# Causal attention with the row maximum carried in spare rows of the score product, and its masking moved to GpSimd

## The chip, the cores and the metric

The kernel runs as one program on one core of a Trainium2 chip. The metric is device time in microseconds of one execution, the median over the runs of the kernel. Engines: TensorE (PE in the rows; PEld is its weight load), VectorE (DVE), ScalarE (ACT), GpSimd (POOL) and the sync engine (SP), which issues the loads and stores.

## The reference, cut to what matters

The model has two layers over 16 sequences of 256 tokens, width 128. Layer 0 is a recurrence and a 64-expert network; layer 1 is attention and a 16-expert network. Only the attention of layer 1 is touched. Head width is 8, there are 16 heads, and since the rotary width is the whole width, only the rotary half of queries and keys is left:

```python
q_r = _apply_rope(x @ wqr + bqr, cos, sin)
k_r = _apply_rope(x @ wkr + bkr, cos, sin)
ckv = _gelu(x @ wkv + bkv)
v = (ckv @ wv + bv).reshape(b, s, H, HD).transpose(0, 2, 1, 3)
q, k = (_gelu(t).reshape(b, s, H, HD).transpose(0, 2, 1, 3) for t in (q_r, k_r))
scores = jnp.einsum('bhqd,bhkd->bhqk', q, k) / math.sqrt(HD)
scores = jnp.where(causal[None, None], -jnp.inf, scores)
attn = jax.nn.softmax(scores, axis=-1)
out = jnp.einsum('bhqk,bhkd->bhqd', attn, v)
return out @ wo + bo
```

## The kernel before, in words

The program runs layer 0, then the expert network of layer 1 (eight token tiles; it also leaves queries and keys in SBUF, feature by token, each split in a high part and a rest: `qh`, `ql`, `kh`, `kl`), then attention, one sequence ("batch") at a time. Every engine's queue is written out by hand and synchronised by named semaphores; nothing is scheduled by a tool. The attention loop is a software pipeline of three stages in each body `both(ba, bx, bo)`: stage A prepares batch b+2, stage X scores and averages batch b+1, stage O finishes batch b. Two parities alternate (`par`).

Stage A, `a_unit` (L1180 ACT, L1334 PE, L1614 DVE), goes through `UNITS` (L971), each unit into PSUM bank 0 or 1 by turns. Units `k` spread four heads at a time over the partitions: head j of a group of four sits on partitions 32j and following. 8 of the 32 partitions carry a head's high part, further ones repeat it or carry the rest, so that one product sums the split terms; the last 8 are spare. ScalarE copies the keys (`kr`, L1188). The query units do the same, and copies masked by `qmask` give each head an own copy of 128 partitions by 256 tokens (`qb`), zero outside its 32 partitions: eight heads by VectorE (L1623), eight by ScalarE (L1192). Units `max0` and `max1` compute scores with queries on partitions, two heads a unit, for the first and the second 128 queries, add the causal mask with a bf16 product of the identity and `mask_b`, and VectorE takes the row maximum (L1628). After the last one VectorE splits the maximum in two parts (`mhl`, L1631 and L1633), unit `mT` transposes them (L1367) and ScalarE copies them to `mT` (L1198).

Stage X: `scores_t` (L1371 and following) computes the transposed scores, keys on partitions, in eight units of two heads. Each of a unit's four quarters takes three products into one accumulation: keys by masked queries, `esel` by `mT` (which subtracts the row maximum), and the causal mask. Units alternate between two pairs of banks. ScalarE takes the exponential of 768 columns (L1204). `values` multiplies four heads' probabilities by values at once (L1398), into banks 6 and 7.

Stage O: ScalarE copies the raw output (L1210), TensorE transposes it (L1409), VectorE divides by the row sums (L1640, L1644), TensorE transposes (L1414), ScalarE copies (L1213), TensorE projects with `wo`, VectorE multiplies by the gate (L1649) and adds the residual (L1653). All plain products are recorded at the helper's line, L1239; the tiles tell them apart. `l_xt` and `l_wqk` hold `kr` of the two parities, `l_big` holds `qb`, the probabilities and small tiles, `l_rope` the raw output, `l_hid` the values.

GpSimd (`pool`, L1090 and following) sets constants, subtracts two splits for each token tile of the expert network and has nothing to do in attention. The sync queue loads layer 1's constants one after the other ahead of the first tile (L990), and the selectors `c_rep` and `c_esel` in four pieces during the last expert tile; VectorE casts each between experts (L1568).

## Time and profile before

| | |
|---|---|
| median of 3 runs | 2396.91 us (2391.91 to 2397.82) |
| profiled execution, own time | 2401.08 us |
| its span | 2399.3 us |
| mean granted TensorE clock | 0.882 |
| busy: TensorE, VectorE, ScalarE, GpSimd | 77%, 67%, 45%, 38% of the span |
| attention stage | 1890.6 us to the end |
| one batch in attention | 30.4 us |

The span is the stretch that the profile covers; the profiled execution's own time is 1.8 us longer. Busy time of TensorE counts overlapping matmuls once, and a matmul's recorded duration includes its way through the array; what one costs in a dense row of them is the distance between two starts. A granted clock of 1.00 is TensorE's higher level, 2.4 GHz; 0.5 would be 1.2 GHz throughout a stretch.

### The profile page before, as it was taken

The page shows a single profiled execution, that of the slowest core. Times are in us where ns is not written, and L with a number is a line of the kernel's source. Part 1 is how long each engine was busy: PE and PEld are TensorE (multiplying, and loading weights), DVE is VectorE, ACT ScalarE, POOL GpSimd, SP SyncE. Part 2 cuts the span into 40 slices and gives each one's busy share as a digit, 9 for nine tenths or more (in the row PEclk, how much of TensorE's full clock was granted, in tenths as well). Part 3 has the DMA queues.
Part 4 walks back from the last instruction along what each step waited for, and adds up shares of the span by engine and source line. Part 5 has one row for each costly group of instructions (what it writes and reads, how often), then busy time and mean ns, then how long its engine had stood idle before and what let it go on. Part 6 is the DMA issues. An engine that isn't in the chain of part 4 may idle for free. (4 is left out here: it accounts for less than half of the span.)

```text
span 2399.3 us, 35571 instructions
## 1 busy us (share of the span) xinstructions
PE 1837.1 (77%) x10242; PEld 1372.1 (57%) x10242; DVE 1615.1 (67%) x4233; ACT 1075.5 (45%) x1779; POOL 910.0 (38%) x729
## 2 busy tenths in 40 slices
PE   1384875866848768477486299898999999999998
PEld 1252553533525435244253288787888777777776
DVE  3599899898997989989989344444444444444443
ACT  2262553643625536355253155454455344444443
POOL 2776775757767667577486100000000000000000
PEclk8697887977978879789798599999999799999999
DMA  6220030200300203002000411111100100000000
GB/s 108 59 49 0 10 49 6 38 17 6 54 1 14 45 6 54 0 5 49 5 5 5 118 21 22 23 23 24 19 14 14 40 8 14 13 13 13 13 13 11
DMA packets 140839, 60.21 MB, mean 25 GB/s; under 512 B 94599, under 2 KB 135036, under 8 KB 140668
## 3 DMA queue, kind: packets, MB, share of 16 engines
q1 hardware_dynamic: 140668, 58.24, 12.0%
q8 instruction: 70, 1.15, 0.2%
q14 instruction: 101, 0.83, 0.1%
HBM read 37.10 MB, written 21.10 MB: 24 GB/s over the span
## 5 line engine op out<-in xcount | busy, mean ns | idle before, releaser
L554 PE MATMUL pb<-hid,wd 128*128 128x512 f32 x528 | 319.8, 691 | 215.6 <-POOL hid L391 211.0
L387 POOL TENSOR_TENSOR hid<-act_g,act_u 128x512 f32<-128x512 f32 x256 | 331.1, 1293 | 277.4 <-ACT act_c L481 260.1
L391 POOL TENSOR_TENSOR hid<-hid,act_c 128x512 f32<-128x512 f32 x256 | 332.7, 1300 | 20.1
L481 ACT ACTIVATE act_g<-pb 128x512 f32<-128x512 f32 (+1 forms) x264 | 158.5, 600 | 389.2 <-PE pb L504 386.1
L1239 PE MATMUL l_pb<-l_xt,l_big 128*128 128x512 f32 (+1 forms) x1024 | 299.4, 415 | 34.6 <-DVE l_rope L1518 24.1
L1586 DVE SCALAR_TENSOR_TENSOR l_acc<-l_pb,l_gtok,l_acc 128x128 f32<-128x128 f32 x512 | 144.0, 344 | 256.8 <-PE l_pb L1239 256.8
L502 PE MATMUL pb<-xt_hi,wg_hi 128*128 128x512 f32 (+1 forms) x264 | 223.9, 848 | 67.0 <-DMA wd<-in_L_ffn_Ws_down_dram 51.1
L554 PEld LDWEIGHTS pb<-hid,wd 128*128 128x128 f32 x528 | 96.6, 208 | 301.6 <-POOL hid L391 280.1
L1239 PEld LDWEIGHTS l_pb<-l_big,l_hid 128*128 128x128 f32 x2048 | 247.1, 192 | 10.6
L1628 DVE TENSOR_REDUCE l_mrow<-l_pb 128x2 f32<-128x256 f32 (+1 forms) x256 | 137.2, 556 | 171.9 <-PE l_pb L1239 168.9
L1167 ACT ACTIVATE l_hid<-l_pb,l_cols 128x512 f32<-128x512 f32 x256 | 169.4, 688 | 183.1 <-PE l_pb L1239 182.7
L1239 PE MATMUL l_pb<-l_big,l_hid 128*128 128x128 f32 x2048 | 247.9, 275 | 0.0
L1239 PEld LDWEIGHTS l_pb<-l_xt,l_big 128*128 128x128 f32 x1024 | 194.6, 200 | 73.0 <-DVE l_rope L1518 22.7
L756 DVE TENSOR_TENSOR products<-zr,rs 128x512 f32<-128x512 f32 x256 | 175.7, 686 | 23.7 <-POOL zr L340 10.4
L1204 ACT ACTIVATE l_big<-l_pb 128x768 f32<-128x768 f32 x128 | 104.6, 817 | 176.0 <-PE l_pb L1398 89.4
L502 PE MATMUL pb<-xt_hi,wu_hi 128*128 128x512 f32 (+1 forms) x264 | 116.3, 441 | 77.8 <-ACT act_g L481 77.7
L759 DVE TENSOR_REDUCE rs<-products 128x32 f32<-128x512 f32 x256 | 175.8, 687 | 0.0
L1105 POOL TENSOR_TENSOR l_ql<-l_rope,l_qh 128x512 f32 x8 | 10.3, 1289 | 434.5 <-ACT l_qh L1161 434.5
L757 DVE TENSOR_TENSOR products<-zr,rs 128x512 f32<-128x512 f32 x256 | 174.1, 680 | 0.0
L481 ACT ACTIVATE act_u<-pb 128x512 f32<-128x512 f32 (+1 forms) x264 | 158.1, 599 | 24.6 <-PE pb L504 16.5
L481 ACT ACTIVATE act_c<-pb 128x512 f32<-128x512 f32 x256 | 153.1, 598 | 0.0
L1239 PE MATMUL l_pb<-l_mT,l_esel 128*128 128x256 f32 x512 | 143.3, 280 | 0.0
(305 smaller groups left out, 4125.4 us busy)
## 6 DMA issues: line engine op xcount, KB each, us to landing
z_scratch<-zs SPq DMA_DIRECT2D x128, 81.0 KB, 4.2
zr<-z_scratch SPq DMA_DIRECT2D x8, 1296.0 KB, 8.4
x_sb<-in_L_attn_x_dram SPq DMA_DIRECT2D x32, 64.0 KB, 3.2
g_scratch<-act_u SPq DMA_DIRECT2D x8, 256.0 KB, 2.3
y_scratch<-yo SPq DMA_DIRECT2D x8, 256.0 KB, 2.3
l_xs<-in_L_attn_x_dram SPq DMA_DIRECT2D x32, 64.0 KB, 1.9
l_ys<-y_scratch SPq DMA_DIRECT2D x128, 16.0 KB, 1.7
l_gs<-g_scratch SPq DMA_DIRECT2D x8, 256.0 KB, 3.0
```

Source lines behind the costliest of these rows:

```text
L387: pool.tensor_tensor(hid1[:, :], g, u, ALU.mult).then_inc(s_h1, 1)
L391: pool.tensor_tensor(hid[:, p % 2, :], hid1[:, :], c, ALU.mult).then_inc(s_h, 1)
L481: act.activation(dst, pb[0:n, r % 4, :], ACT.Silu if what == 0 else ACT.Copy).then_inc(s_ev, 1)
L502: pe.matmul(out, l_hi, r_hi, start=first, stop=False, skip_group_check=True)
L554: last = pe.matmul(pb[:, 4, :], wd[0:n, p, :], hid[0:n, p % 2, :], start=(p == 0), stop=(p == PAIRS), skip_group_check=True)
L756: dve.tensor_tensor(products[:, 2:4], two(ZG), twice, ALU.mult).then_inc(s_st, 1)
L757: dve.tensor_tensor(products[:, 0:2], two(ZF), twice, ALU.mult).then_inc(s_st, 1)
L759: dve.tensor_reduce(rs[:, 3, 0:2], products[:, 2:4], AX.X, ALU.add).then_inc(s_st, 1)
L1167: act.activation(hid[:, r % HR, :], pb[:, 2 + r % 3, :], ACT.Relu, bias=cols[:, r:r + 1]).then_inc(s_hid, 1)
L1239: return pe.matmul(out, l, r, start=start, stop=stop, skip_group_check=True)
L1586: dve.scalar_tensor_tensor(out=acc[:, s, :], in0=pb[:, 5 + e % 2, sub], scalar=gtok[par][:, s, e:e + 1], in1=acc[:, s, :], op0=ALU.mult, o ...
L1628: dve.tensor_reduce(mrow[:, k, 2 * j:2 * j + 2], src, AX.X, ALU.max).then_inc(s_ua_dve, 1)
```

## The change

The masked copies change sides and engine. Queries are copied unmasked (`qr`) by VectorE; keys are copied by ScalarE with a bias `kspare` that puts -1 in two spare rows of each head's 32. GpSimd makes masked copies of the keys (`kb`, used by the maximum pass with four or two heads side by side in 512 columns) and of the queries (`qb`, used by the transposed scores). The maximum pass has twelve units instead of sixteen: for each group of four heads one with the first 128 queries and 128 keys of all four, and two with the second 128 queries and 256 keys of two heads; the mask is added in one product per unit. They use banks 2 and 3. The maximum's two parts are transposed to partitions 32j and 32j+1, in eight transposes, and copied straight into those rows of `qb`, groups j = 0 and 1 by ScalarE and j = 2 and 3 by VectorE. So the score product subtracts the maximum itself: `esel` and `mT` go, with their load, and so does the mask product. A score unit is one product of 512 columns (first 128 keys, two heads, all queries) and one of 256 (second 128 keys and queries), into banks 4 and 5 for every unit. The exponential is unchanged in size; after it GpSimd writes zeros above the diagonal with two `affine_select` per unit, and only then may `values` read. Ahead of each group of its work GpSimd does a one-column product on a small tile, the "turnstile".

```diff
         qb = [b[:, :].rearrange("p (h n) -> p h n", h=H1) for b in (big0, big1)]
-        kr = xt[0][:, :, :].rearrange("p a n -> p (a n)"), wqk[:, :, :, :].rearrange("p a j n -> p (a j n)")
+        GN = 4 * N
+        kr = xt[0][:, :, :].rearrange("p a n -> p (a n)"), wqk[:, :, :, :].rearrange("p a j n -> p (a j n)")[:, 0:GN]
+        qr = xt[1][:, :, :].rearrange("p a n -> p (a n)")
+        kb = sb("kb", [P, H1, N], F32R)
...
-        esel = sb("esel", [P, H1, P], F32R)
...
+        kspare = sb("kspare", [P, 1])
...
+        pt2 = sb("pt2", [P, 4, 3 * N])
         mrow = sb("mrow", [P, 2, H1])
-        mhl = sb("mhl", [P, 2, P], F32R)
-        mT = [sb(f"mT{i}", [P, N], F32R) for i in range(2)]
+        mhl = sb("mhl", [P, 2, H1, 32], F32R)
...
+        def probs(u):
+
+            p = (pt, pt2)[u // 4][:, u % 4, :]
+            return p[:, 0:2 * N].rearrange("p (m n) -> p m n", m=2), p[:, 2 * N:3 * N].rearrange("p (m n) -> p m n", m=2)
...
-        UNITS = ["k"] * 2 + ["q_dve", "q_act"] + ["max0"] * 8 + ["max1"] * 8 + ["v", "mT"]
+        UNITS = ["k0", "q0", "k1", "q1"] + ["max"] * 12 + ["v", "m"]
...
+        BY_ACT = [u in ("k0", "k1", "v") for u in UNITS]
+        BY_DVE = [u in ("q0", "q1", "max") for u in UNITS]
...
+        MAX0, NM, XU = 4, 12, 8
+        X_AT, V_AT = (2, 3, 5, 6, 8, 9, 11, 12), (7, 10, 13, 16)
+
+        O_RAW, O_TB, O_NORM, O_OT, O_WO, O_END = 0, 1, 2, 4, 5, 6
...
+        def max_rows(par, j):
+
+            rows = qb[par][32 * j:32 * j + 2, :, :].rearrange("p (g j) n -> p g j n", j=4)
+            return rows[:, :, j, :]
...
+            w(kspare[:, :], d["c_kspare"])
...
-            for i in range(4):
...
-                sp.dma_start(rep_stage, d[("c_rep", "c_esel")[i // 2]][:, STAGED * (i % 2):STAGED * (i % 2 + 1)]).then_inc(s_rep_ld, 16)
+                sp.dma_start(rep_stage, d["c_rep"][:, STAGED * i:STAGED * (i + 1)]).then_inc(s_rep_ld, 16)
...
+            def turn(n):
+                pool.wait_ge(s_turn, n)
+                pool.tensor_tensor(turnstile[:, 1:2], turnstile[:, 0:1], turnstile[:, 0:1], ALU.mult).then_inc(s_turn, 1)
...
+            def masked_keys(b, par, half, turns):
+
+                pool.wait_ge(*read(b, 2 * half))
+                turn(turns)
+                for j in range(4):
+                    at = slice(2 * N * half, 2 * N * (half + 1))
+                    out = kb[:, 8 * half:8 * (half + 1), :].rearrange("p (g j) n -> p g j n", j=4)[:, :, j, :]
+                    src = kr[par][:, at].rearrange("p (g n) -> p g n", n=N)
+                    last = pool.tensor_scalar(out, src.bitcast(F32), qmask[:, j:j + 1], None, ALU.mult)
+                last.then_inc(s_kb, 1)
...
+            def masked_queries(b, par, half, turns):
...
+            def causal(b, u, turns):
+
+                pool.wait_ge(s_pt, b * XU + u + 1)
+                turn(turns)
+                for k in range(2):
+                    diagonal = probs(u)[k][:, :, 0:P]
+                    last = pool.affine_select(diagonal, diagonal, pattern=[[0, 2], [1, P]], base=0, channel_multiplier=-1,
+                                              compare_op=ALU.is_ge, fill=0.0)
+                last.then_inc(s_cut, 1)
...
+            def both(ba, bx, pa, turns):
+                done = 0
+                for i in range(NU):
+                    if bx is not None and i - 1 in X_AT:
+                        causal(bx, X_AT.index(i - 1), turns + done)
+                        done += 1
+                    if ba is not None and i in (1, 2):
+                        masked_keys(ba, pa, i - 1, turns + done)
+                        done += 1
+                    if ba is not None and i in (8, 12):
+                        masked_queries(ba, pa, i // 12, turns + done)
+                        done += 1
...
+                if u[0] == "k":
+                    act.wait_ge(s_ua, b * NU + (i + 1))
+                    at = 2 * N * int(u[1])
+                    act.activation(kr[par][:, at:at + 2 * N], pb[:, BANK[i], :], ACT.Identity, bias=kspare[:, :]).then_inc(s_ua_act, 1)
...
+                elif u == "m":
+                    act.wait_ge(s_ua, b * NU + (i + 1))
+                    act.wait_ge(s_qb, (b + 1) * 2)
+                    for j in range(2):
+                        last = act.activation(max_rows(par, j), pb[32 * j:32 * j + 2, 0:2, :].rearrange("p a (g n) -> p (a g) n", n=N), ACT.Copy)
+                    last.then_inc(s_mq[0], 1)
...
             def x_unit(b, par, u):
+
                 act.wait_ge(s_st, b * XU + (u + 1))
-                act.wait_ge(s_pv, b * (XU // 2) + max(u // 2 - 1, 0))
-                at = 512 * (2 + 2 * (u % 2)) + N
-                act.activation(pt[:, u % 4, :], pbf[:, at:at + 3 * N], ACT.Exp, scale=float(1.0 / np.sqrt(HD1))).then_inc(s_pt, 1)
+                if u == 0:
+                    act.wait_ge(s_pv, b * 4)
+                p = (pt, pt2)[u // 4][:, u % 4, :]
+                act.activation(p, pbf[:, 4 * 512:4 * 512 + 3 * N], ACT.Exp, scale=float(1.0 / np.sqrt(HD1))).then_inc(s_pt, 1)
...
-                    if bx is not None and i % 2 == 0 and i // 2 < XU:
-                        x_unit(bx, px, i // 2)
+                    if bx is not None and i in X_AT:
+                        x_unit(bx, px, X_AT.index(i))
...
+                if u == "max":
+                    m = i - MAX0
+                    g, part = m // 3, m % 3
+                    if m >= 2:
+                        pe.wait_ge(*read(b, i - 2))
+                    if part == 0 and g % 2 == 0:
+                        pe.wait_ge(*read(b, g + 1))
+                        pe.wait_ge(s_kb, b * 2 + g // 2 + 1)
+                    bank = pb[:, 2 + m % 2, :]
+                    if part == 0:
+                        mm(bank.rearrange("p (j n) -> p j n", j=4), qr[:, N * g:N * g + P], kb[:, 4 * g:4 * (g + 1), 0:P], stop=False)
+                        last = mm(bank.rearrange("p (j n) -> p j n", j=4), ident_b[:, :], mask_b[:, :].unsqueeze(1).to_broadcast([P, 4, P]), start=False)
+                    else:
+                        h = 4 * g + 2 * (part - 1)
+                        mm(bank, qr[:, N * g + P:N * (g + 1)], kb[:, h:h + 2, :].rearrange("p h n -> p (h n)"), stop=False)
+                        last = mm(bank.rearrange("p (j n) -> p j n", j=2)[:, :, P:N], ident_b[:, :], mask_b[:, :].unsqueeze(1).to_broadcast([P, 2, P]), start=False)
+                    last.then_inc(s_ua, 1)
+                    return
+                bank = pb[:, BANK[i], :]
+                if u == "m":
+                    pe.wait_ge(s_mhl, b + 1)
+                    pe.wait_ge(*read(b, NU - 2))
+                    for h in range(0, H1, 4):
+                        for k in range(2):
+                            src = mhl[:, k, h:h + 4, :].rearrange("p j c -> p (j c)").bitcast(F32)
+                            at = N * (h // 4) + P * k
+                            last = pe.transpose(pbf[:, at:at + P], src, ident[:, :])
+                    last.then_inc(s_ua, 1)
+                    return
...
             def scores_t(b, par, u):
 
-
                 if u == 0:
-                    pe.wait_ge(s_ua_act, (b + 1) * N_ACT)
-                    pe.wait_ge(s_pt, b * XU)
-                elif u >= 2:
-                    pe.wait_ge(s_pt, b * XU + (u - 1))
-                bank = 512 * (2 + 2 * (u % 2))
-                for k, m, lo in ((1, 1, N), (1, 0, P), (0, 0, 2 * N), (0, 1, 3 * N)):
-                    h = 2 * u + m
-                    keys = N * (h // 4) + P * k
-                    out = pbf[:, bank + lo:bank + lo + N]
-                    mm(out, kr[par][:, keys:keys + P], qb[par][:, h, :], stop=False)
-                    mm(out, esel[:, h, :], mT[par][:, :], start=False, stop=False)
-                    last = mm(out[:, P * k:P * (k + 1)], mask_b[:, :], ident_b[:, :], start=False)
+                    for n in range(2):
+                        pe.wait_ge(s_mq[n], b + 1)
+                pe.wait_ge(s_pt, b * XU + u)
+                g, heads = u // 2, slice(2 * u, 2 * u + 2)
+                mm(pb[:, 4, :], kr[par][:, N * g:N * g + P], qb[par][:, heads, :].rearrange("p h n -> p (h n)"))
+                last = mm(pb[:, 5, 0:N].rearrange("p (m n) -> p m n", m=2), kr[par][:, N * g + P:N * (g + 1)], qb[par][:, heads, P:N])
                 last.then_inc(s_st, 1)
...
-            def values(b, par, u):
-
-                pe.wait_ge(s_pt, b * XU + (u + 2))
-                if u == 0:
+            def values(b, par, g):
+
+                pe.wait_ge(s_cut, b * XU + 2 * (g + 1))
+                if g == 0:
                     pe.wait_ge(s_done, b)
-                out = pb[:, 6 + u // 4, N * (u // 2 % 2):N * (u // 2 % 2 + 1)]
+                out = pb[:, 6 + g // 2, N * (g % 2):N * (g % 2 + 1)]
...
+                        p = probs(2 * g + m // 2)[k][:, m % 2, :]
+                        last = pe.matmul(out[VC * m:VC * (m + 1), P * k:N], vp[par][:, k, 4 * g + m, :], p, start=(k == 0), stop=(k == 1),
...
+                    if bx is not None and i in X_AT:
+                        scores_t(bx, px, X_AT.index(i))
+                    if bx is not None and i in V_AT:
+                        values(bx, px, V_AT.index(i))
...
+                if u == "m":
+                    dve.wait_ge(s_ua, b * NU + (i + 1))
+                    dve.wait_ge(s_qb, (b + 1) * 2)
+                    for j in range(2, 4):
+                        last = dve.tensor_copy(max_rows(par, j), pb[32 * j:32 * j + 2, 0:2, :].rearrange("p a (g n) -> p (a g) n", n=N))
+                    last.then_inc(s_mq[1], 1)
...
+                if u[0] == "q":
+                    at = 2 * N * int(u[1])
+                    dve.tensor_copy(qr[:, at:at + 2 * N], pb[:, BANK[i], :]).then_inc(s_ua_dve, 1)
...
+                m = i - MAX0
+                g, part = m // 3, m % 3
+                if part == 0:
+                    dst, heads = mrow[:, 0, 4 * g:4 * (g + 1)], 4
+                else:
+                    dst, heads = mrow[:, 1, 4 * g + 2 * (part - 1):4 * g + 2 * part], 2
+                dve.tensor_reduce(dst, pb[:, 2 + m % 2, :].rearrange("p (j n) -> p j n", j=heads), AX.X, ALU.max).then_inc(s_ua_dve, 1)
...
-                    dve.tensor_copy(mhl[:, :, 0:H1], mrow[:, :, :]).then_inc(s_mc, 1)
...
+                    dve.tensor_tensor(mhl[:, :, :, 1], mrow[:, :, :], mhl[:, :, :, 0].bitcast(F32), ALU.subtract).then_inc(s_mhl, 1)
...
-                    rep[h * HD1 + i, kind, h // 4, 32 * (h % 4) + HD1 * part + i] = 1
+                    rep[h * HD1 + i, kind, h // 4, 32 * (h % 4) + HD1 * (part + 1) + i] = 1
...
+    spare = np.zeros((4, 32), f)
+    spare[:, 0:2] = -1
+    c["c_kspare"] = spare.reshape(P, 1)
```

**GpSimd's queue**, one body of the attention loop in the changed program (from its start up to the last masked copy; each select pair stands with the turnstile ahead of it; before, the queue had nothing here):

```order
L1140 TENSOR_TENSOR l_turnstile<-l_turnstile 128x1 [waits a_turnstile]
L1152 TENSOR_SCALAR l_kb<-l_xt,l_qmask 128x2x256 x4
...
L1139 REGISTER_ALU [waits a_probs_exp]
L1140 TENSOR_TENSOR l_turnstile<-l_turnstile 128x1 [waits a_turnstile]
L1172 AFFINE_SELECT l_big<-l_big 128x2x128
L1172 AFFINE_SELECT l_big<-l_big 128x256
...
L1139 REGISTER_ALU [waits a_unit_read_by_dve]
L1140 TENSOR_TENSOR l_turnstile<-l_turnstile 128x1 [waits a_turnstile]
L1163 TENSOR_SCALAR l_big<-l_xt,l_qmask 128x2x256 x4
```

In one body the sequence is: two key maskings, four select pairs, a query masking, three select pairs, a query masking, one select pair.

**TensorE's queue**, a score unit of the attention loop before (`l_big` the masked queries, `l_wqk` the keys; a unit has four such groups of three):

```order
L1239 REGISTER_ALU [waits a_unit_read_by_act]
...
L1239 MATMUL l_pb<-l_big,l_wqk 128x256 [waits a_probs_ready]
L1239 MATMUL l_pb<-l_mT,l_esel 128x256
L1239 MATMUL l_pb<-l_ident_b,l_mask_b 128x128
L1239 MATMUL l_pb<-l_big,l_wqk 128x256
L1239 MATMUL l_pb<-l_mT,l_esel 128x256
L1239 MATMUL l_pb<-l_ident_b,l_mask_b 128x128
```

and the end of a body in the changed program, from the last score unit on (L1323 is the helper's line now, L1490 `values`, L1447 the maximum's transposes):

```order
L1323 MATMUL l_pb<-l_big,l_xt 128x512 [waits a_probs_exp]
L1323 MATMUL l_pb<-l_big,l_xt 128x256
...
L1490 MATMUL l_pb<-l_pt,l_hid 32x256 [waits a_probs_causal]
...
L1323 MATMUL l_pb<-l_wv,l_big 128x128 [waits a_latent_copied,a_unit_read_by_act]
L1323 MATMUL l_pb<-l_wv,l_big 128x128
L1447 MATMUL l_pb<-l_ident,l_mhl 128x128 [waits a_unit_read_by_act,a_max_split]
L1447 MATMUL l_pb<-l_ident,l_mhl 128x128 x7
```

A score unit went from twelve products to two; a value group now waits for GpSimd's selects, and the maximum's transposes stand behind the last value group and the value projection.

## Rows read from the trace of the kernel before

**Rows 1.** The page: busy us by engine (share of the span) xinstructions.
```profile
PE 1837.1 (77%) x10242; PEld 1372.1 (57%) x10242; DVE 1615.1 (67%) x4233; ACT 1075.5 (45%) x1779; POOL 910.0 (38%) x729
```

**Rows 2.** Twelve batches: length, busy us PE, PEld, DVE, ACT, POOL, clock, DMA, GB/s.
```profile
2008.90:2373.10 364.20, 346.16 (x3168) 284.16 (x3168) 152.46 (x300) 152.19 (x276) 0.00 (x0) 1.00 0.05 13
```

**Rows 3.** The longest TensorE wait of one batch: us in total, times, longest.
```profile
PE l_pb L1239 <- DVE l_big L1623: 0.7, 1, 0.7
```

**Rows 4.** TensorE timeline (start, us, instruction), then two pieces of the chain.
```profile
2101.37 0.28 PE L1239 MATMUL l_pb<-l_mT,l_esel 128*128 128x256 f32 x1
2101.48 0.23 PE L1239 MATMUL l_pb<-l_ident_b,l_mask_b 128*128 128x128 bf16 x1
2101.52 0.36 PE L1239 MATMUL l_pb<-l_kh,l_rep 128*128 x1
2101.72 0.28 PE L1239 MATMUL l_pb<-l_kl,l_rep 128*128 x1
...
2108.23 0.23 PE L1239 MATMUL l_pb<-l_mask_b,l_ident_b 128*128 128x128 bf16 x1
...
2108.48 0.23 PE L1239 MATMUL l_pb<-l_mask_b,l_ident_b 128*128 128x128 bf16 x1
...
1885.61 1.65 PE L1239 MATMUL l_pb<-l_xt,l_big 128*128 128x512 f32 x6
1887.10 0.27 PE L1239 MATMUL l_pb<-l_big,l_hid 128*128 128x128 f32 x1
...
2097.79 0.79 PE l_pb L1398 x16
...
2102.24 0.87 PE l_pb L1409 x8
```

**Rows 5.** Groups by line and shape, 1900 to 2300 us: busy us, mean ns, idle before.
```profile
L1204 ACT ACTIVATE l_big<-l_pb 128x768 f32<-128x768 f32 x101 | 82.6, 818 | 138.9 <-PE l_pb L1398 71.6 <-PE l_pb L1239 67.3
...
L1628 DVE TENSOR_REDUCE l_mrow<-l_pb 128x2 f32<-128x512 f32 x104 | 67.4, 687 | 55.1 <-PE l_pb L1239 55.1
...
L1623 DVE TENSOR_TENSOR l_big<-l_pb,l_qmask 128x1024 fp32r<-128x1024 f32 x26 | 30.6, 1220 | 87.4 <-PE l_pb L1239 87.4
...
L1210 ACT ACTIVATE l_rope<-l_pb 128x1024 f32<-128x1024 f32 x12 | 12.3, 1022 | 0.1
...
L1188 ACT ACTIVATE l_wqk<-l_pb 128x512 fp32r<-128x512 f32 x14 | 8.4, 598 | 10.8 <-PE l_pb L1239 10.5
...
L1653 DVE TENSOR_TENSOR l_ys<-l_ys,l_xs 128x256 f32<-128x256 f32 x12 | 5.1, 426 | 1.5
```

**Rows 6.** Groups by line and shape, GpSimd, whole span; columns as in rows 5.
```profile
L369 POOL TENSOR_TENSOR wu_lo<-act_g,wu_hi 128x1024 fp32r<-128x1024 f32 x1 | 2.4, 2350 | 0.1
...
L367 POOL TENSOR_SCALAR wu_hi<-act_c 128x1024 fp32r<-128x1024 f32 x1 | 1.0, 1043 | 0.0
...
L369 POOL TENSOR_TENSOR wu_lo<-act_c,wu_hi 128x64 fp32r<-128x64 f32 x1 | 0.3, 319 | 0.1
...
L367 POOL TENSOR_SCALAR wu_hi<-act_c 128x64 fp32r<-128x64 f32 x1 | 0.2, 245 | 0.0
```

**Rows 7.** Windows of layer 0, columns as in rows 2.
```profile
840.00:900.00 60.00, 37.53 (x107) 22.36 (x106) 49.80 (x126) 20.58 (x37) 37.14 (x31) 0.74 0.02 6
1260.00:1320.00 60.00, 37.42 (x117) 20.13 (x115) 55.72 (x136) 22.46 (x39) 38.26 (x31) 0.81 0.02 5
```

**Rows 8.** Timeline, first batch; the maximum's copies, first and last start; a sync-queue load.
```profile
1890.59 0.36 PE L1239 MATMUL l_pb<-l_kh,l_rep 128*128 128x256 f32 x1
...
1895.21 0.41 PE L1239 MATMUL l_pb<-l_qh,l_rep 128*128 128x256 f32 x1
1895.42 0.41 PE L1239 MATMUL l_pb<-l_ql,l_rep 128*128 128x256 f32 x1
...
L1198 ACT ACTIVATE l_mT<-l_pb x16: 384/384/384, 1916.1 to 2373.1; 128x256 fp32r<-128x256 f32 x16
...
1326.45 0.42 SPq L990 DMA_DIRECT2D l_qmask<-in_c_qmask_dram  x1
```

132 lines of the change are left out of this document (55 added, 77 removed).

## The prediction

> **What bounds the kernel now.** I read the page first: TensorE is the busiest engine of the span (1837 of 2399 us), but the change touches only the attention stage, from the first head-spreading product at 1890.6 us to the end of the span, and one short load [rows 1, 8]. I then took that stage by windows. Twelve consecutive batches take 364.20 us, 30.35 us each, with TensorE busy 95% of it at the full granted clock and GpSimd at nothing [rows 2]. VectorE and ScalarE are busy 12.7 us of a batch each. So a batch is TensorE's list of work plus short waits; in the list of waits of one batch its longest is 0.7 us, for VectorE's query copies [rows 3].
>
> Matmul durations overlap, so I price each by start to start. A score group of three (score, maximum, mask) steps by 0.36 us; in it the maximum takes 0.11 up to the mask, the mask 0.04, and the product that follows a mask 0.20. A 256-column product that follows another of its kind costs what the maximum does, about 0.12. A pair of the maximum pass (score, mask) steps by 0.25 from mask to mask, 0.245 over longer rows of them [rows 4]. Per batch: 32 groups are 11.5 us, 32 pairs 7.8, sixteen spreading products 1.9, four value groups at 0.79 are 3.2, the output's transposes and projection about 2.0, the rest 0.6. That is 27.0 of 30.35.
>
> **What goes from TensorE.** The scores become eight units of one 512-column and one 256-column product. A 512-column product steps by 0.25 us (six in 1.49) [rows 4], so a unit is 0.25 + 0.12 = 0.37 and all eight 3.0 instead of 11.5. The maximum pass has twelve units: four with a 512-column product and a 512-column mask, eight with a 512-column product and a 256-column mask. I take a mask for no dearer than a product of its width: 4 x 0.50 + 8 x 0.37 = 5.0 instead of 7.8. The maximum's transposes grow from 2 to 8, which take 0.87 as the eight output transposes do [rows 4]. TensorE's list falls to about 16 us. It stops being the bound, so the saving is not 11 us: the question is what comes next.
>
> **VectorE and ScalarE.** VectorE: twelve 512-element reductions at 0.686 are 8.2, two query copies of 512 about 0.65 each instead of 2.4, and two new copies of 1024 elements from two partitions, at most the 1.22 of the masked 1024-element copy, 2.4. With what it keeps, about 14. ScalarE loses eight masked copies and gains two 1024-element copies at 1.02; with eight exponentials at 0.82 it stays near 12 [rows 5]. Neither reaches 16 us; their place in the chain matters, not their sum.
>
> **GpSimd gets a full list.** Per batch sixteen masked copies of 512 elements, sixteen selects of 256, twelve one-column products, in one queue. Masked copy: the one-input TENSOR_SCALAR takes 244 ns at 64 columns and 1042 at 1024, so 0.62 at 512; neighbours overlap by about 0.04, so 0.58: 9.3 us. One-column product: the two-input line (319 ns at 64 columns, 2350 at 1024) goes back to 0.19, less the overlap 0.15: 1.8 us. AFFINE_SELECT is nowhere in this trace. Lower bound, the one-input line at 256 elements: 0.40. Upper bound, the two-input line at 256: 0.72. It has one input but a comparison besides, so I take the middle, 0.56, 0.52 by its start: 8.4 us [rows 6]. With half a microsecond of gates the list is 20.1 us.
>
> **The ring that sets the batch.** The order of the queues shows it. GpSimd's last select of a batch gates the last value group; behind that on TensorE stand the value projection and the maximum's transposes; their copies into the queries gate the next key product; that product's copy gates GpSimd's first masking. Nothing of GpSimd's list can start earlier. The steps: four key products at 0.12 and the last one's drain of 0.28, 0.76, and their copy 0.60, with gates 1.5; GpSimd 20.1; value group 0.79, projection 0.24, transposes 0.87 and drain 0.3, together 2.2; VectorE's two copies 2.4 [rows 4 to 6]. That is 26.2 us. A second path is nearly as long: from 2.4 us eight rounds of score unit, drain, exponential and gate (0.37 + 0.25 + 0.82 + 0.05) with three value groups between, 14.3, then the last four reductions with their products 3.6 and the split 0.4, hence the same transposes at 20.7 where the first path has its last select at 21.6. If selects were free, this one would hold the batch at about 25.5.
>
> **The clock.** TensorE will be busy about 60% of the time. Where it was busy 62% of a stretch in this trace it was granted 0.74 to 0.81 of full speed, at 95% it was granted 1.00 [rows 2, 7]; in the low level (1.2 GHz of 2.4) a spreading product steps by 0.21 instead of 0.12 [rows 8]. The ring holds about 2.7 us of TensorE, in the low level up to twice that; with the low level for half of it, and some from the second path, I add 1.15. A batch: **27.35 us**, 3.0 less.
>
> The Trainium skill, "SBUF — State Buffer", section "Who interferes with whom", speaks against moving work to GpSimd: a VectorE instruction with two SBUF inputs contends with a GpSimd one that reads SBUF, and the later one fully blocks. VectorE has two such per batch, the maximum's short split and the last addition (0.43) [rows 5]. GpSimd stands idle beside them here, so no row shows it; if each waited a whole 0.62 instruction, that would be 1.2 us a batch and 18 us in all, off the ring for the greater part. I leave it out of the sum and inside the range.
>
> **Ends of the stage.** The first batch has no scores beside it: before, 25.5 us up to its maximum's copy [rows 8]. Now key copy, one masking of two and twelve reductions at about 0.9 in the low clock, split, transposes and copies: about 21.5, 4 less. The last two bodies took 26 us [rows 8]; eight exponential rounds with four value groups and the unchanged output path take as much, plus 1 for the clock. One more load on the sync queue ahead of the layer costs its issue, about 0.45 [rows 8]. Two fewer selector loads and casts lay behind the experts' products and cost nothing; they would only show if TensorE waited there, and it does not.
>
> **The sum**: the profiled execution took 2401.1. Fifteen batches by 3.0 are 45, first batch 4, against 1.5 back: 2353.6. The median of the runs is 4.2 under the profiled one, so **2349 us**.
>
> **Rivals.**
> 1. *The select is dear, and GpSimd holds the batch above 30.35.* Sixteen a batch for fifteen batches turn each 0.1 us of price into 24 us. The forecast's 47.5 is gone at 0.56 + 0.20 = 0.76, barely above the two-input row. For it: an unseen instruction, and two-input arithmetic already costs 2.1 ns an element here. Against it: one input. At 1.0 a batch is 34.4 and the time 2455; at 1.3 it is 2527. The Trainium skill, "GPSIMD Engine Reference", section 3.1, says that data-dependent branching costs about 12 cycles an element; by that, at its 1.2 GHz, a select would be an estimated 2.6 us and the time near 2840, and no row here shows such an instruction. Chance 0.30, slower.
> 2. *The low clock makes TensorE the bound again.* Its 16 us become about 28 where each product costs 1.75 times (0.21 for 0.12), and with the copies it cannot cover (2.4) a batch is back at 30.4: 2396. For it: idle stretches bring the low level. Against: a TensorE that is the bound is busy, and busy stretches had 1.00. Chance 0.08.
> 3. *The select is as cheap as the one-input row, 0.40.* Then the second path holds, 25.5 to 26 us a batch: about 2320. Chance 0.10.
> That the change does not shorten TensorE's list is excluded by the order: per batch 32 maximum products and 32 score masks are gone from its queue.
>
> **How the numbers follow.** Forecast 0.52, rivals 0.30, 0.08, 0.10. The measurement tells 0.3%, 7 us, from no change. Faster: 0.52 + 0.10 + a quarter of rival 2 = 0.64; same 0.04; slower 0.32. The range starts at rival 3 with the full clock, 2315, and goes up to a select of 1.0 us, 2455; above lies what is left of rival 1. The forecast's own range, a select of 0.44 to 0.72, is 2320 to 2388.
>
> **What would show it.** Right: a batch of 26 to 28.5 us; GpSimd busy without a gap from the first masking to the last select and idle 6 us; TensorE's longest waits on the causal semaphore ahead of value groups; masked copies of 0.62; granted clock 0.7 to 0.85 after 1915 us. Wrong: a select above 0.76; TensorE waiting rather on exponentials or reductions; masked copies above 0.7 (each 0.1 costs 24 us too); VectorE's 1024-element copies on two partitions well off 1.2.

## The result and the profile after

The changed kernel takes 2584.64 us (median of 4, 2578.24 to 2589.09) against 2394.77 of the kernel before beside it: ratio 1.079, 95% interval 1.076 to 1.082. It is slower by 8%, where I had forecast 2% faster, and lies above the range's end of 2455.

The page of the changed kernel; columns as in [rows 1], and the granted clock by 40 slices:
```profile
span 2587.4 us, 32711 instructions
...
PE 1781.3 (69%) x8418; PEld 1267.9 (49%) x8418; DVE 1650.6 (64%) x4199; ACT 1060.5 (41%) x1667; POOL 1429.1 (55%) x1434
...
PEclk7797978979788796987958999999977777776767
```
GpSimd has 519 us more than in [rows 1]. The attention stage is the last quarter of the slices, and there the clock is down to 6 and 7 tenths from 9 in the slices just before it (in the kernel before, the same stage had 1.00 [rows 2]).

The length of one batch, laid from the fourth masked copy of a batch's keys on, and the stage, by windows; columns as in [rows 2]:
```profile
2099.63:2141.90 42.27, 26.04 (x149) 17.32 (x148) 14.21 (x23) 11.75 (x16) 32.14 (x45) 0.67 0.03 9
1900.00:2560.00 660.00, 397.43 (x2268) 269.40 (x2268) 229.59 (x356) 180.35 (x243) 505.68 (x677) 0.72 0.03 8
```
A batch takes 42.27 us (the maximum's splits start 15 batches apart at 1913.3 and 2547.3) where it took 30.35 [rows 2] and was to take 27.35. GpSimd works 32.1 of it, TensorE 26.0, and the two elementwise engines what I had given them (14.2 and 11.8). So GpSimd's list and something of 10 us outside it make the batch. Its groups by shape, 1900 to 2560 us, then the two on VectorE and ScalarE that stand on the ring:
```profile
L1163 POOL TENSOR_SCALAR l_big<-l_xt,l_qmask 128x512 fp32r<-128x512 f32 x128 | 198.5, 1578 | 0.0
L1152 POOL TENSOR_SCALAR l_kb<-l_wqk,l_qmask 128x512 fp32r<-128x512 f32 x64 | 99.1, 1567 | 0.0
...
L1172 POOL TENSOR_SCALAR_AFFINE_SELECT l_big<-l_big 128x256 f32<-128x256 f32 x120 | 46.5, 415 | 0.0
L1140 POOL TENSOR_TENSOR l_turnstile<-l_turnstile 128x1 f32<-128x1 f32 x183 | 37.3, 204 | 146.0 <-ACT l_wqk L1270 75.1 <-ACT l_xt L1270 70.8
...
L1710 DVE CAST l_big<-l_pb 2x1024 fp32r<-2x1024 f32 x32 | 39.2, 1226 | 132.9 <-PE l_pb L1447 125.7 <-POOL l_big L1163 7.0
...
L1279 ACT ACTIVATE l_big<-l_pb 2x1024 fp32r<-2x1024 f32 x32 | 32.4, 1014 | 39.8 <-PE l_pb L1447 32.1 <-POOL l_big L1163 7.5
```
Here is the surprise. The instruction that I had feared, the select, costs 0.415, near the one-input end of its bounds. The one that I had priced from a row and not feared, the masked copy, costs 1.57 instead of 0.62.

The timeline between two lists of GpSimd, in order of start (the weight loads, the small key products, TensorE's and ScalarE's output work left out):
```profile
2126.44 0.77 POOL L1172 TENSOR_SCALAR_AFFINE_SELECT l_pt<-l_pt 128x256 f32<-128x256 f32 x2
2127.26 1.51 PE L1490 MATMUL l_pb<-l_pt,l_hid 128*32 128x256 f32 x16 [4.42 <-POOL l_pt L1172]
2128.70 1.22 PE L1323 MATMUL l_pb<-l_wv,l_big 128*128 128x128 f32 x4
2129.96 0.38 ACT L1273 ACTIVATE l_hid<-l_pb 128x256 f32<-128x256 f32 x1 [9.50 <-PE l_pb L1323]
2130.40 1.97 PE L1447 MATMUL l_pb<-l_ident,l_mhl 128*128 128x128 f32 x8 [0.47 <-ACT l_hid L1273]
2132.49 2.04 ACT L1279 ACTIVATE l_big<-l_pb 2x1024 fp32r<-2x1024 f32 x2 [2.14 <-PE l_pb L1447]
2132.50 2.46 DVE L1710 CAST l_big<-l_pb 2x1024 fp32r<-2x1024 f32 x2 [8.28 <-PE l_pb L1447]
...
2135.21 0.58 PE L1323 MATMUL l_pb<-l_kh,l_rep 128*128 x1 [2.85 <-DVE l_big L1710]
...
2136.47 0.69 ACT L1270 ACTIVATE l_xt<-l_pb,l_kspare 128x512 fp32r<-128x512 f32 x1 [0.59 <-PE l_pb L1323]
2137.33 0.19 POOL L1140 TENSOR_TENSOR l_turnstile<-l_turnstile 128x1 f32<-128x1 f32 x1 [10.12 <-ACT l_xt L1270]
```
Each bracket names the row above it as releaser: last select, value group, value projection, transposes, the maximum's copies, next key product, its copy, first masking. That is the ring of the prediction, with one more step in it: the transposes (L1447) wait 0.47 for ScalarE's copy of v (L1273), since they write PSUM bank 0, out of which it reads. Ahead of that gap GpSimd works through its list without a pause: from 1950 us to 2560 us it waits for nothing but the key copies, 14 times, 141.2 us.

### The profile page after: what moved, and what is told of

Its sections match the earlier page's. It is cut to its first block and busy times, and to the rows that moved or that the text cites. A ratio compares the mean times of both kernels' runs of the same rounds, so it can differ in the third digit from the quotient of the medians.

```text
span 2587.4 us, 32711 instructions
## 1 busy us (share of the span) xinstructions
PE 1781.3 (69%) x8418; PEld 1267.9 (49%) x8418; DVE 1650.6 (64%) x4199; ACT 1060.5 (41%) x1667; POOL 1429.1 (55%) x1434
## 5 line engine op out<-in xcount | busy, mean ns | idle before, releaser
L391 POOL TENSOR_TENSOR hid<-hid,act_c 128x512 f32<-128x512 f32 x256 | 332.1, 1297 | 20.1
L1725 DVE TENSOR_REDUCE l_mrow<-l_pb 128x2 f32<-128x512 f32 (+1 forms) x192 | 131.1, 690 | 198.4 <-PE l_pb L1323 196.1
L1323 PEld LDWEIGHTS l_pb<-l_big,l_hid 128*128 128x128 f32 x2048 | 247.1, 192 | 10.5
L1323 PE MATMUL l_pb<-l_big,l_hid 128*128 128x128 f32 x2048 | 247.9, 275 | 0.0
L1323 PE MATMUL l_pb<-l_xt,l_big 128*128 128x512 f32 x768 | 220.6, 422 | 26.3 <-DVE l_rope L1608 24.4
L1163 POOL TENSOR_SCALAR l_big<-l_xt,l_qmask 128x512 fp32r<-128x512 f32 x128 | 198.5, 1578 | 0.0
L481 ACT ACTIVATE act_u<-pb 128x512 f32<-128x512 f32 (+1 forms) x264 | 158.3, 600 | 25.5 <-PE pb L504 17.3
L1323 PEld LDWEIGHTS l_pb<-l_xt,l_big 128*128 128x128 f32 x768 | 139.4, 195 | 57.0 <-DVE l_rope L1608 23.0
L1140 POOL TENSOR_TENSOR l_turnstile<-l_turnstile 128x1 f32<-128x1 f32 x192 | 39.1, 203 | 165.3 <-ACT l_wqk L1270 75.1
```

What stands on the lines that cost most here:

```text
L391: pool.tensor_tensor(hid[:, p % 2, :], hid1[:, :], c, ALU.mult).then_inc(s_h, 1)
L481: act.activation(dst, pb[0:n, r % 4, :], ACT.Silu if what == 0 else ACT.Copy).then_inc(s_ev, 1)
L1163: last = pool.tensor_scalar(out, src.bitcast(F32), qmask[:, j:j + 1], None, ALU.mult)
L1323: return pe.matmul(out, l, r, start=start, stop=stop, skip_group_check=True)
```

## The experiments

A time without a ratio beside it is that of one execution; the six of the fastest version below lie within 1.0% of each other. A batch is the distance from the first to the last start of the maximum's split, divided by 15.

**Which property of the masked copy is dear?** My first theory was its factor, which is a column of qmask (a pointer) where the row it was priced from has a number. Rivals: the strided output, the neighbours (a port shared with VectorE), the number of arithmetic operations. The first run puts twelve forms one after another on GpSimd before attention, each waiting for the one before it.

```diff
+ for form in range(12):
+     ...    # 0, 1: tensor_scalar(out, src, 1.0, 1.0, mult, mult), 1 and 2 with a strided output
+            # 2: tensor_scalar(out, src, 1.0, None, mult); 3, 4: the same with qmask[:, 0:1]
+     i_.then_inc(s_pr, 1); pool.wait_ge(s_pr, n_pr)
```


> The changed kernel with a list of probes on GpSimd, twelve forms four times over, put where its queue is idle before attention (each waits for the one before; 512 elements a partition unless said). Theory A (the per-partition factor): a TENSOR_SCALAR whose factor is a number takes about 0.62 us in both layouts of the output, and the one whose factor is read from a column of SBUF takes about 1.57 us even here, where no attention work runs beside it; 128 columns of that form about 0.45. Rival B (the layout: two pieces of 256 a stride of 1024 apart): the number-factor copy into the strided output takes 1.57 too, the column-factor copy into 512 adjoining elements 0.62. Rival C (contention with the attention work of the other engines): every one-input form takes about 0.62 here. Beside these: the product with a broadcast column 1.07 to 1.3, the plain product of two tensors 1.3, a plain copy 0.6, a select of 512 about 0.65. The kernel's time stays within 0.5% of the changed kernel's 2585 us.

The timeline of the probes, all on GpSimd (start, us, instruction), one round:
```profile
1402.57 0.62 POOL L1134 TENSOR_SCALAR l_kb<-l_pt 128x512 fp32r<-128x512 f32 x1
1403.28 0.62 POOL L1136 TENSOR_SCALAR l_kb<-l_pt 128x512 fp32r<-128x512 f32 x1
1403.98 1.49 POOL L1138 TENSOR_SCALAR l_kb<-l_pt 128x512 fp32r<-128x512 f32 x1
1405.57 1.57 POOL L1140 TENSOR_SCALAR l_kb<-l_pt,l_qmask 128x512 fp32r<-128x512 f32 x1
1407.24 1.57 POOL L1142 TENSOR_SCALAR l_kb<-l_pt,l_qmask 128x512 fp32r<-128x512 f32 x1
...
1409.59 1.04 POOL L1146 TENSOR_TENSOR l_kb<-l_pt,l_qmask 128x512 fp32r<-128x512 f32 x1
1410.69 0.61 POOL L1148 CAST l_kb<-l_pt 128x512 fp32r<-128x512 f32 x1
1411.37 0.61 POOL L1150 CAST l_kb<-l_pt 32x512 fp32r<-32x512 f32 x1
1412.07 1.48 POOL L1152 TENSOR_SCALAR l_kb<-l_pt 32x512 fp32r<-32x512 f32 x1
```
L1134 and L1136 multiply by a number twice, contiguous and strided: 0.62, the price of my row. L1138 multiplies by a number once: 1.49. With a column (L1140, L1142) it is 1.57, contiguous or strided alike. No attention work runs beside them. The expert network does (in the 13 us of this round TensorE is busy throughout, VectorE 6.2 us, ScalarE 4.9), but the prices hardly depend on it: in four rounds the one-operation forms are within 0.01 of the values above, and so are those with two, but for one that took 1.06. So neither the attention work nor chance makes the difference. The form with **one** operation is 2.4 times as dear as the form with **two**; the pointer adds 0.08, the layout nothing, and 32 partitions cost what 128 do (L1150, L1152). The whole kernel stays at 2585.09 us, so the probes lie outside its path.

**The factor alone**, in the kernel itself:
```diff
- last = pool.tensor_scalar(out, src.bitcast(F32), qmask[:, j:j + 1], None, ALU.mult)
+ last = pool.tensor_scalar(out, src.bitcast(F32), 0.25, None, ALU.mult)
```


> All sixteen masked copies of a batch multiply by the number 0.25 in place of the mask column, so heads are not kept apart and the output is not attention; shapes, order and waits are as they were. Theory A with the ring: a copy falls from 1.55 us by start to 0.58, GpSimd's list of a batch from 31.9 to about 16.5 us, the batch from 42.3 to about 27 (the path over scores and exponentials may hold it at 28), the time to 2340 to 2375 us. Rivals B and C: the copies stay at 1.55, the time at 2585. Rival D (the copies are cheaper but TensorE in its low clock level is what holds the batch): the copies fall to 0.58 and the batch stays above 33, the time above 2440.

Measured 2560.71 us; the copies 1.49, a batch 40.81 ((2517.0 - 1904.9) / 15). The pointer was worth 24 us of 190. That theory falls.

**The selects out**, the value groups waiting for the exponentials instead (the one-column product of each select is kept):
```diff
-     last = pool.affine_select(diagonal, diagonal, ...)
- last.then_inc(s_cut, 1)
...
- pe.wait_ge(s_cut, b * XU + 2 * (g + 1))
+ pe.wait_ge(s_pt, b * XU + 2 * (g + 1))
```


> The selects are taken out (probabilities above the diagonal are not set to zero, so the output is not causal attention); the one-column products stay, and a value group waits for the exponentials alone. The ring: GpSimd's list loses sixteen selects, 5.8 us by their starts (the last one alone ends the list ahead of the last value group), the batch falls to about 36.5, the time by 87 to about 2498 us; the last query masking, and no value group, then stands ahead of the maximum's copies. Rival D (TensorE, exponentials or reductions hold the batch): the time stays within 20 us of 2585.

Measured 2424.24 us, a batch 32.16: 10.1 less, though the sixteen selects are only 5.8 us of the list (eight pairs, 0.73 from a pair's start to the next row), and 4.3 less than the 36.5 that I had expected, a miss. GpSimd's idle time fell as well, from 10.1 to 5.3 us a batch (it works 250.24 of 300 us), because the last value group no longer has a select to wait for and so moves off the ring with the projection and the transposes. (The clock rose with it, from 0.72 to 0.88 in 2000 to 2300 us; what that gave is not taken apart.) The selects' *place*, in front of those steps, costs nearly as much as their time.

**Copies of 32 partitions into a zeroed background**, so that no mask is read at all, each with its own one-column product:
```diff
+ rows_j = slice(32 * j, 32 * (j + 1))
+ pool.wait_ge(s_turn, turns + 2 * j)
+ pool.tensor_tensor(turnstile[rows_j, 1:2], ...)
+ pool.tensor_scalar(out[rows_j], src.bitcast(F32)[rows_j], 1.0, None, ALU.mult)
```


> Same computation. The masked copies become plain copies of the 32 partitions that belong to the head, into buffers set to zero once; a one-column product on the same partitions carries the wait ahead of each copy. Theory A: a copy takes about 0.6 us, its companion and two gates 0.3; GpSimd's list is 16 x 0.9 + 5.8 + 1.3 + gates, about 22 us instead of 31.9, the batch about 32, the time about 2430 us, still slower than the kernel before (2395). If the price of a copy hangs on the number of partitions and falls below 0.4 us, about 2380. Rivals B and C: the copies stay at 1.55, the list grows by the waits to about 37, the time to about 2660.

Measured 2663.04 us, ratio 1.110 (1.106 to 1.114). A copy on a quarter of the partitions costs 1.482, hardly less than the whole; with the added waits a batch takes 47.02. That is the time that I had given the rivals, not my theory of the factor: with a number for a factor the copies stayed dear.

**Two operations instead of one.** If the number of operations is the cause, a second multiplication by 1.0 must take most of the loss away:
```diff
- last = pool.tensor_scalar(out, src.bitcast(F32), qmask[:, j:j + 1], None, ALU.mult)
+ last = pool.tensor_scalar(out, src.bitcast(F32), qmask[:, j:j + 1], 1.0, ALU.mult, ALU.mult)
```


> Same computation: the masked copies multiply by the mask column and then by 1.0, two operations in place of one. Theory E (after the first runs: a GpSimd TENSOR_SCALAR with one operation takes the dear 2.9 ns an element, with two the cheap 1.1, and where the factor comes from hardly matters): the copy falls from 1.55 us by start to about 0.6, GpSimd's list of a batch from 31.9 to about 17, the rest of the ring stays 10.2, the batch is about 27.3, the time about 2358 us (2335 to 2385), so faster than the kernel before. Rival A' (a factor read from a column forbids the cheap form): the copy stays at 1.5, the time at 2585. Rival D (the low clock, exponentials or reductions hold the batch once the copies are cheap): the copy is 0.6 and the batch stays above 29, the time above 2385.

Measured **2371.63 us**, ratio to before 0.989 (0.985 to 0.993), and a batch of 28.88: one extra operand turns 8% slower into 1% faster. Its groups, columns as above:
```profile
L1163 POOL TENSOR_SCALAR l_big<-l_xt,l_qmask 128x512 fp32r<-128x512 f32 x120 | 80.7, 690 | 0.0
...
L1172 POOL TENSOR_SCALAR_AFFINE_SELECT l_pt<-l_pt 128x256 f32<-128x256 f32 x128 | 48.9, 406 | 0.0
```
The copies are at 0.69, and the price of nothing else on GpSimd moved. The batch is 1.6 longer than the 27.3 that I expected of it, and GpSimd's queue shows where:
```profile
2112.43 0.19 POOL L1140 TENSOR_TENSOR l_turnstile<-l_turnstile 128x1 f32<-128x1 f32 x1 [0.68 <-ACT l_xt L1270]
...
2124.87 0.19 POOL L1140 TENSOR_TENSOR l_turnstile<-l_turnstile 128x1 f32<-128x1 f32 x1 [1.25 <-ACT l_pt L1288]
```
With cheap copies its list has gaps: it waits for the second key copy (0.68, in the batch before 1.20) and for the exponential of the seventh score unit (1.25). From the first masking to the last select it takes 20.6 us, where I had expected 17; the rest of the ring takes 8, where I had expected 10.2. The same kernel with eight more forms probed on the idle GpSimd:

> The same kernel with a second list of probes on GpSimd's idle queue ahead of attention, eight forms four times over, 512 elements each. Theory E: column factor and number 1.0, both products, 0.62 in either layout; two column factors at most 0.7; number product and number sum 0.62; one operation stays dear, 1.48, whether it is a sum or a product and whether the output is fp32 or rounded. Rival A': every form with a column factor takes about 1.5. Rival F (the rounding of the output makes it dear): the one-operation copies into fp32 take 0.62.

```profile
1396.68 0.69 POOL L1134 TENSOR_SCALAR l_kb<-l_pt,l_qmask 128x512 fp32r<-128x512 f32 x1
1397.46 0.70 POOL L1136 TENSOR_SCALAR l_kb<-l_pt,l_qmask 128x512 fp32r<-128x512 f32 x1
1398.27 0.77 POOL L1138 TENSOR_SCALAR l_kb<-l_pt,l_qmask 128x512 fp32r<-128x512 f32 x1
1399.12 0.62 POOL L1140 TENSOR_SCALAR l_kb<-l_pt 128x512 fp32r<-128x512 f32 x1
1399.83 1.50 POOL L1142 TENSOR_SCALAR l_kb<-l_pt 128x512 fp32r<-128x512 f32 x1
...
1403.00 1.57 POOL L1146 TENSOR_SCALAR l_pt<-l_pt,l_qmask 128x512 f32<-128x512 f32 x1
1404.67 0.69 POOL L1148 TENSOR_SCALAR l_pt<-l_pt,l_qmask 128x512 f32<-128x512 f32 x1
```
Column and number 0.69, strided 0.70, column and column 0.77, number with multiply and add 0.62: each column adds 0.08, whatever the operations. One addition alone (L1142) is 1.50 like one multiplication, and an fp32 output (L1146, L1148) changes nothing. That run took 2363.84 us.

**Two other ways to the same copy**: casts on 32 partitions (0.603 each, with the gates of the 32-partition version), and a two-input multiplication by the broadcast column:
```diff
+ pool.tensor_copy(out[rows_j], src.bitcast(F32)[rows_j])                                  # q_cast
+ last = pool.tensor_tensor(out, src.bitcast(F32), qmask[:, j:j + 1].unsqueeze(2).to_broadcast([P, 2, N]), ALU.mult)   # e_tt
```


> Same computation. As the earlier run with plain copies of each head's own 32 partitions into zeroed buffers, but with the copy instruction, which the first probes had at 0.61 us, in place of the one-operation TENSOR_SCALAR at 1.48. A copy with its one-column companion and two gates is 0.92; GpSimd's list about 22 us, the batch about 32.5, the time about 2435 us. If the ring is not what holds the batch (rival D), the time falls by less than 120 us from that run's 2663.

> Same computation: the masked copy is a product with the mask column repeated along the row (TENSOR_TENSOR, 1.04 us in the first probes). GpSimd's list 31.9 - 16 x 0.53 = 23.4, the batch about 33.7, the time about 2453 us. It lies between the changed kernel and the run with two operations, so the three together show whether the batch follows GpSimd's list one for one.

The casts gave 2395.96 us, ratio 0.999 (0.997 to 1.001), a batch of 30.05; that is well under what I had expected of them, a miss. From one cast to the next in its timeline it is only 0.81 us, wait and one-column product included. The multiplications gave 2459.21 with copies of 1.04 and a batch of 33.63, as expected. From the two-operation version to this one the sixteen copies grow by 5.6 us (0.35 each) and the batch by 4.75; from here to the changed kernel by 8.5 (0.53 each) and 8.6. So a batch follows GpSimd's list one for one over the dear half, and a little less at the cheap end, where the gaps shown above open in the list.

**What is left of the ring.** The two-operation version still leaves GpSimd idle for 7.8 us a batch. Its timeline there, instructions that waited:
```profile
2101.13 0.86 PE L1490 MATMUL l_pb<-l_pt,l_hid 128*32 128x256 f32 x16 [0.93 <-POOL l_pt L1172]
2102.66 0.38 ACT L1273 ACTIVATE l_hid<-l_pb 128x256 f32<-128x256 f32 x1 [4.84 <-PE l_pb L1323]
2103.10 1.09 PE L1447 MATMUL l_pb<-l_ident,l_mhl 128*128 128x128 f32 x8 [0.47 <-ACT l_hid L1273]
...
2107.05 0.38 PE L1323 MATMUL l_pb<-l_kh,l_rep 128*128 x1 [2.85 <-DVE l_big L1710]
...
2108.89 0.19 POOL L1140 TENSOR_TENSOR l_turnstile<-l_turnstile 128x1 f32<-128x1 f32 x1 [7.82 <-ACT l_xt L1270]
```
Two of its steps are there by choice. The transposes share banks 0 and 1 with the copy of v and the next key and query products; and the last value group stands in front of them, so that they wait for the last select although they don't need it. Two edits of the two-operation version take these out:
```diff
  # e_bank: transposes to banks 2 and 3, the first maximum products wait for the copies instead
- pe.wait_ge(*read(b, NU - 2))
...
- at = N * (h // 4) + P * k
+ at = 2 * 512 + N * (h // 4) + P * k
...
- pb[32 * j:32 * j + 2, 0:2, :]
+ pb[32 * j:32 * j + 2, 2:4, :]
  # e_late: the last value group behind the transposes
- if bx is not None and i in V_AT:
+ if bx is not None and i in V_AT[:3]:
...
+ if bx is not None:
+     values(bx, px, 3)
```


> The changed kernel with two operations in the masked copy (median 2371.63 us, batch 28.88 us by the first maximum splits 1899.8 and 2333.0) and the eight transposes of the maximum moved from banks 0 and 1 to banks 2 and 3. Theory A (the ring over GpSimd sets the batch and the copies of the maximum and of v stand on it): the transposes no longer wait for ScalarE's copy of v (0.47 us) and the next key product (1.22 us at the low clock, 0.6 at the high one) runs beside the copies of the maximum, so 1.1 to 1.7 us a batch, batch 27.2 to 27.8, time 2347 to 2356 us. Theory B (scores and exponentials set it by now, with the ring at the same length only by their waits): batch 28.6 to 28.9, time 2367 to 2372.

> The kernel with two operations in the masked copy, and on TensorE the last group of value products put behind the transposes of the maximum. Theory A (ring): the transposes stop waiting for the last pair of selects (0.9 us) and for the value group itself (0.8 to 1.5 us), so 1.2 to 2.0 us a batch, batch 26.9 to 27.7, time 2342 to 2354 us. Theory B (second path): the exponentials of the next batch wait for the value group, which now comes later, batch 28.5 to 29.5, time 2366 to 2381.

> Both edits together on the kernel with two operations in the masked copy. Theory A (ring): the gains add until GpSimd's list (some 20.5 us with gates) or the second path (25.5 us by the prediction, 26.5 with the clock at 0.9) is the bound: batch 26.0 to 27.0, time 2328 to 2344 us, below the kernel before by 50 to 65 us. Theory B: no more than the better of the two single edits, within 5 us.

| version (two operations) | median us | ratio to before (95%) | batch us | clock, 2000 to 2300 |
|---|---|---|---|---|
| as it is | 2371.63 | 0.989 (0.985 to 0.993) | 28.88 | 0.90 |
| banks 2 and 3 | 2342.43 | 0.978 (0.974 to 0.982) | 27.21 | 0.94 |
| value group last | 2334.46 | 0.974 (0.970 to 0.978) | 26.28 | 0.96 |
| both | **2319.58** | **0.970 (0.966 to 0.974)** | 25.89 | 0.97 |

Theory A (the ring) holds, and both single edits gave more than its band of times. With the banks moved the batch stands at the low end of what was expected; with the value group last it is 0.6 below it, and the clock's rise from 0.90 to 0.96 goes that way, though I have not taken the two apart. Together they don't add: 25.89 is 3.0 below, where the single edits are 1.7 and 2.6; it is still a little under the 26.0 to 27.0 that I expected. The timeline of the version with both shows why:
```profile
2134.90 1.11 DVE L1753 TENSOR_TENSOR l_ys<-l_ys,l_xs 128x256 f32<-128x256 f32 x1
...
2136.16 0.86 PE L1491 MATMUL l_pb<-l_big,l_hid 128*32 128x256 f32 x16 [1.73 <-DVE l_ys L1753]
...
2147.68 1.09 PE L1449 MATMUL l_pb<-l_ident,l_mhl 128*128 128x128 f32 x8 [0.82 <-DVE l_mhl L1733]
2148.89 2.04 ACT L1279 ACTIVATE l_big<-l_pb 2x1024 fp32r<-2x1024 f32 x2 [1.61 <-PE l_pb L1449]
...
2153.02 0.19 POOL L1140 TENSOR_TENSOR l_turnstile<-l_turnstile 128x1 f32<-128x1 f32 x1 [5.72 <-ACT l_wqk L1270]
```
The transposes now wait for the maximum's split, and no longer for a select or for v: the second path of the prediction (scores, exponentials, last reductions), which I had put at 25.5. It has a stretch that I had not counted: the first value group (L1491) waits 1.73 for VectorE's residual addition (L1753), which ends the output stage of the batch before. That my 25.5 is so near is therefore luck in part.

The last run puts both edits on the changed kernel as it is, with its one-operation copies:

> The changed kernel as it is (one operation in the masked copy, batch 42.28 us of which GpSimd works 31.9 and stands idle 10.1), with both reorderings: the transposes of the maximum in banks 2 and 3, and the last group of value products behind them. Theory A (one ring, whose part outside GpSimd runs at the low clock and is what these two edits take out): GpSimd's idle time falls to ScalarE's two copies of the maximum (2.0 us) and the key copy (0.7) less the last pair of selects and its gates (1.0), so about 2 us, and the batch to 34 to 36 us, time 2470 to 2500 us. Theory B (the reorderings are worth what they were worth in the version with two operations, 3.0 us a batch): batch 39.3, time about 2540 us.

Measured 2485.03 us, a batch of 36.08 ((2452.9 - 1911.7) / 15), its clock 0.83. GpSimd waits 3.3 and 3.7 us a batch instead of 10.1 (I expected 2):
```profile
2101.37 0.19 POOL L1140 TENSOR_TENSOR l_turnstile<-l_turnstile 128x1 f32<-128x1 f32 x1 [3.30 <-ACT l_xt L1270]
```
The same edits that save 3.0 beside the cheap copies save 6.2 here. Where GpSimd's list is the bound, the whole of what they take from the ring counts; where it isn't, the second path catches the batch after three.

## Why the prediction was wrong

**The step that failed is the price of the masked copy**: "the one-input TENSOR_SCALAR takes 244 ns at 64 columns and 1042 at 1024, so 0.62 at 512". [Rows 6] are right and the interpolation too; the probes give 0.62 for that form. But line 367, which made those rows, multiplies twice (`1.0, 1.0, ALU.mult, ALU.mult`), and the change's line multiplies once (`qmask[:, j:j + 1], None, ALU.mult`). Both show in the trace as TENSOR_SCALAR; only the code tells them apart. Four copies take 6.19 us by the timeline instead of 2.32: 15.5 us a batch. I named the size of the danger ("masked copies above 0.7 (each 0.1 costs 24 us too)") and gave it no chance and no bound from above.

**The other terms, batch by batch.** Forecast 27.35, measured 42.27, 14.9 more:
- Masked copies: +15.5. One-column products 0.15: right.
- Selects 0.52 by their start, measured 0.37 (0.73 for a pair): -2.5. The true price was rival 3's, "as cheap as the one-input row", a case with a chance of 0.10. Rival 1 forecast the sign, with the wrong instruction: it had "GpSimd holds the batch above 30.35", for a dear select.
- Gates in the list, 0.5: hardly there. (With them my terms give 20.0 for the list, where I wrote 20.1.)
- The ring outside GpSimd, forecast at 6.1 and 1.15 for the clock, is 10.1 measured: +2.9. From start to start in the timeline above: value group 1.44 for 0.79, projection with its drain 1.26 for 0.24, copy of v 0.44 for nothing, transposes with their drain 2.10 for 1.17, the maximum's copies 2.71 for 2.4, key products with their drain 1.26 for 0.76, key copy 0.86 for 0.74. From 2127.0 us to 2137.3 us the granted clock was 0.50. In the two-operation version it is 7.8 to 8.1, so there my sum was 0.6 to 0.9 short.

These add up to 15.4, half a microsecond too much: the batch that they are read from is 42.5 long where the mean is 42.27, and the rest is rounding.

**The clock** was forecast at 0.7 to 0.85 and is 0.72. I had the level right, and took too little for it: I put "the low level for half" of the ring's 2.7 us, and it was all of them, with the drains behind them (0.50 in that stretch, as above).

**TensorE's list.** 32 groups gone, TensorE no longer the bound, 26.0 us busy of 42.3 at the low clock: right. Rival 2 (TensorE the bound again) did not come; it is idle 16 us of a batch.

**Ends of the stage.** From the first key product to the maximum's copies 29.7 us (1891.2 to 1920.9), where I said 21.5; from the last such copies to the end 30.5, where I said 27. The first holds masked copies at 1.57; the second has none of them, and its granted clock is 0.72 where the same stretch had 0.95 before. With fifteen batches of 15 us too little they account for the 236 us between the forecast of the profiled execution, 2353.6, and what it took.

**VectorE beside GpSimd.** The maximum's split, by line: duration min/median/max in ns, first and last start:
```profile
L1728 DVE CAST l_mhl<-l_mrow x16: 355/420/803, 1913.3 to 2547.3; 128x32 fp32r<-128x32 f32 x16
L1730 DVE TENSOR_TENSOR l_mhl<-l_mrow,l_mhl x16: 215/646/647, 1913.6 to 2547.8; 128x32 fp32r<-128x32 f32 x16
```
Both take 0.2 undisturbed (0.196 and 0.216 in the two-operation version) and up to 0.80 and 0.65 here. The Trainium skill, "SBUF — State Buffer", section "Who interferes with whom", has the subtraction block for a whole GpSimd instruction; by that rule it could take up to an estimated 1.8 here (0.22 and a copy of 1.57), and the trace shows 0.65 at most. It costs nothing in the time, as the transposes start 6 us after the split (2124.2 to 2130.4). The other such instruction, the last addition, took 0.43 before [rows 5] and takes 0.60 here (median; 0.82 at most), off the ring as I had said. In the version with both reorderings it is on the path: 0.85 in the median and up to 1.12, with the first value group waiting for it as shown above.

With the one wrong row put right, 15 x 15.5 and 4 for the first batch on the forecast give about 2586, within 0.1% of the result; that it is so near is luck, for the cheap selects and the dear ring cancel in it. The order of the ring held, and it is what found the version at 2319.58 us, faster than both kernels. Its sum holds less well: with the measured prices (copies 0.66 from start to start, pairs 0.73) it gives an estimated 25.6 for the two-operation version (10.6 + 5.8 + 1.8 + 6.1 + 1.15), which takes 28.9. Missing are the gaps in GpSimd's list, some 2.2, and most of the rest in the ring outside it.

## What to carry to other kernels

Price an instruction from a row with the same *form*, not only the same name and shape: open the line that made the row and compare operand by operand, including how many operations it does; where they differ in anything, that term has no upper bound yet. When one engine's list stands in a ring with others, ask of every step behind it whether it needs what it waits for: two reorderings that removed no instruction were worth 52 us here, as much as the change was meant to bring. And where a TENSOR_SCALAR on GpSimd has one operation, try a second, idle one: here, on 512 fp32 columns, it more than halved the time.

## What the hardware showed that I had not expected

- GpSimd, 512 columns of fp32: TENSOR_SCALAR with one operation 1.49 us, with two 0.62; each column factor 0.08 more; CAST 0.61; TENSOR_TENSOR 1.04; the select mostly 0.61 (0.40 at 256). A quarter of the partitions takes the same time. The Trainium skill, "GPSIMD Engine Reference", section 4.1, calls one-input work on this engine roughly line-rate, and section 3.1 gives 769 ns measured for 512 elements in its best loop. The two-operation form and the cast agree with the first, and are quicker than the second; the one-operation form, twice the second, agrees with neither. Why it is slow no run here shows.
- Data-dependent branching, by the Trainium skill, "GPSIMD Engine Reference", section 3.1, some 12 cycles an element, was my dearest case for the select. At 0.40 for 256 columns the select shows nothing of it.
- TensorE's busy share alone does not give the granted clock. In 2000 to 2300 us TensorE was busy 214.06 us in the two-operation version and 214.63 with both reorderings, the same share, and was granted 0.90 and 0.97. The version with the shorter ring, and shorter waits of TensorE in it, had the higher clock; no run here separates the two.
